# Graph layer, first aggregation: the three histogram steps and the transposes are issued at other places of the tile

## The reference, cut to what matters

```
src = concat(edges[:, 0], edges[:, 1]);  dst = concat(edges[:, 1], edges[:, 0])
deg = segment_sum(ones, dst)             # how many edges end at each node
deg = maximum(deg, 1.0)
agg = segment_sum(x[src], dst) / deg[:, None]
```

## Time and profile before

| | |
|---|---|
| median of 3 runs | 2717.78 us (2715.9 to 2719.15) |
| the profiled execution | 2714.45 us, of which its span is 2712.4 us |
| first aggregation in the trace | from about 509 us to about 1295 us |
| TensorE busy over the span | 2209.7 us (81%) |
| VectorE busy over the span | 1646.6 us (61%) |
| mean granted TensorE clock | 0.955 |

### The profile page before, as it was taken

One profiled execution on the slowest core, in us unless ns is written; L12 is line 12 of the kernel. 1 busy time (PEld: TensorE's weight loads), 2 busy tenths in 40 slices (PEclk: granted clock), 3 DMA queues, 4 the chain that ended last, 5 costly groups with the idle time before them and its releaser, 6 DMA issues.

```text
span 2712.4 us, 51544 instructions
## 1 busy us (share of the span) xinstructions
PE 2209.7 (81%) x15108; PEld 1359.0 (50%) x15109; DVE 1646.6 (61%) x4628; ACT 909.4 (34%) x1775; POOL 272.7 (10%) x368
## 2 busy tenths in 40 slices
PE   3556666599999999999899997999999968999900
PEld 2444444355555555555455553444444437888800
DVE  6999998687887888788332322444444444555533
ACT  1122221245455544545444442111111114555400
POOL 1000000100000000000110100111111120000076
PEclk9999998899999999999899998999999988999955
DMA  2111110022222222222221214444445534222244
GB/s 76 31 30 35 34 33 29 39 106 98 106 104 103 106 98 106 100 106 104 81 89 44 73 47 167 181 181 180 180 180 181 182 132 166 91 89 93 85 149 135
DMA packets 122211, 281.61 MB, mean 104 GB/s; under 512 B 29659, under 2 KB 65340, under 8 KB 119972
## 3 DMA queue, kind: packets, MB, share of 16 engines
q1 hardware_dynamic: 107107, 230.04, 23.4%
q0 software_dynamic: 15040, 50.81, 5.6%
HBM read 149.42 MB, written 131.33 MB: 104 GB/s over the span
## 4 chain that ended last, share of the span: by engine, by line
PE 49%; DVE 17%; issue 16%; DVEq 7%; POOL 4%; POOLq 2%; ACT 1%; DMA 1%; SPq 1%; ACTq 0%
PE bank L1931 31%; DVE big L1155 6%; PE bank L2141 6%; PE bank L2127 5%; PE bank L1922 3%; POOL big L865 3%; DVEq L1014 2%; POOLq L752 2%; DVE big L1001 2%; DVE big L991 1%; ACT big L1646 1%; DVEq L1020 1%; DVEq L1000 1%; PE bank L2111 1%; DVEq L987 1%
## 5 line engine op out<-in xcount | busy, mean ns | idle before, releaser
L1931 PE MATMUL bank<-RW,big 128*128 128x512 f16 (+1 forms) x4900 | 1180.3, 380 | 0.0
L1931 PEld LDWEIGHTS bank<-RW,big 128*128 128x128 f16 x4900 | 443.9, 98 | 396.2 <-issue 3.6
L1641 ACT ACTIVATE big<-bank 128x512 f16<-128x512 f32 (+1 forms) x640 | 372.0, 581 | 404.9 <-PE bank L1922 404.7
L1155 DVE TENSOR_TENSOR big<-iotaB,keys 128x512 f16<-128x512 f16 x1300 | 456.9, 419 | 24.8 <-PE bank L1922 16.9
L1922 PE MATMUL bank<-big 128*128 128x128 f16 x2560 | 248.3, 219 | 12.0 <-DVE big L1155 11.8
L1922 PEld LDWEIGHTS bank<-big 128*128 128x128 f16 x2560 | 190.9, 98 | 123.9 <-DVE big L1155 13.0
L1764 ACT ACTIVATE big<-bank,b1A,iscA 128x256 f32<-128x256 f32 x224 | 114.4, 561 | 153.5 <-PE bank L2127 153.5
L2127 PE MATMUL bank<-big,RW 128*128 128x256 f16 x1344 | 156.9, 274 | 0.5 <-issue 0.5
L2141 PE MATMUL bank<-RW,big 128*128 x1344 | 156.4, 273 | 0.0
L1807 PE MATMUL bank<-big 128*128 128x100 f16 x980 | 88.8, 282 | 66.4 <-issue 63.7
L2127 PEld LDWEIGHTS bank<-big,RW 128*128 x1344 | 132.1, 98 | 16.5 <-issue 0.7
(11 more groups left out here) (363 smaller groups left out, 2576.0 us busy)
## 6 DMA issues: line engine op xcount, KB each, us to landing
big<-a_dram SPq DMA_DIRECT2D x49, 832.0 KB
big<-a_dram SPq DMA_DIRECT2D x49, 768.0 KB, 4.3
a_dram<-big SPq DMA_DIRECT2D x49, 640.0 KB, 3.0
a_dram<-big SPq DMA_DIRECT2D x49, 512.0 KB, 2.6
a_dram<-big SPq DMA_DIRECT2D x49, 448.0 KB, 2.5
big<-rows_dram SPq DMA_DIRECT2D x56, 256.0 KB, 2.6
y_dram<-big SPq DMA_DIRECT2D x56, 256.0 KB, 2.0
big<-in_x_dram SPq DMA_DIRECT2D x96, 128.0 KB, 2.1
```

Source lines behind the costliest of these rows:

```text
L1155: last = v.tensor_tensor(out[q].rearrange("p b (m k) -> p b m k", k=2), inturn(iotaB[:, :], QB, P // 2), twice(kd[:, q * QB:(q + 1) * QB, ...
L1641: a.activation(Ab[q][:, 0:n], banks[BB(q)][:, 0:n], ACT.Copy).then_inc(s_ab, 1)
L1931: last = mm(bank[:, :], blk(q, c), src, start=(u == 0), stop=(u == T))
```

## The change

Five conditions in the two hand-written orders are changed; no instruction is added, removed or altered. With q the step after which a piece is issued:

| piece | engine | before | after |
|---|---|---|---|
| `paired` (mask) | VectorE | 5 | 2 |
| `fold` | TensorE | 4 | 5 |
| `spread` | VectorE | 8 | 7 |
| `degrees` (sum) | TensorE | 7 | 8 |
| `degree` (reciprocal) | VectorE | 11 | 10 |
| `transposed` of the previous tile | TensorE | 10 | 11 |

`hist` stays behind step 1 of TensorE.

```diff
 # VectorE, tile1
-                        if q == 5:
+                        if q == 2:
                             paired(early)
-                        if q == 8:
+                        if q == 7:
                             spread(early)
-                        if q == 11:
+                        if q == 10:
                             degree(early)
 # TensorE, tile1
                     if q == 1:
                         hist(t)
-                    if q == 4:
+                    if q == 5:
                         fold(t)
-                    if q == 7:
+                    if q == 8:
                         degrees(t)
-                    if q == 10 and last:
+                    if q == 11 and last:
                         transposed(t - 1)
```

## The result

The changed kernel takes 2648.26 us (four runs, 2646.12 to 2650.37) where the kernel before takes 2716.84 (four, 2715.69 to 2719.15): a ratio of 0.9747, 95% interval 0.973 to 0.9763, 68.6 us less. The forecast was 2649.8, from 68 us less than the 2717.78 that three runs of the kernel before had given. The profiled execution of the changed kernel is the slowest of its four, 2650.37 us with a span of 2647.7.

The account below looks back on a forecast made before the run. TensorE was taken as the bound, idle only while `fold` waits for VectorE's mask; 48 tiles times 1.42 to 1.43 us is 68 us, so the median goes from 2717.78 to 2649.8 us, range 2643 to 2662.

Parts of the forecast that it names:

- One wait: Aggregation tiles 1 to 48: TensorE's `fold` waits for VectorE's mask, 59.7 us in 48 times, its only wait there.
- the upper bound: Wait of `fold`: at most 1.41 + 0.04 = 1.45 us a tile, a gain of 69.6 us over 48 tiles.
- the middle: Wait of `fold`: 1.42 to 1.43 us a tile taken, the middle of the upper two values, 68 us over 48 tiles.
- The small matmuls: The two matmuls of `fold` on TensorE: 0.09 us for the pair when nothing waits, 0.045 each.
- its layout: Both engines' new order timed from TensorE's first `build` of a tile: next tile at 14.40 us, TensorE never waiting.
- the two handovers called tight: On VectorE's queue: `degrees` to `degree`, about 0.2 us to spare, and transposes to `place1`, about 0.1.
- the one at line 1188: VectorE's `degree` needs TensorE's `degrees`: about 0.2 us to spare; a wait of 0.1 to 0.3 would cost nothing.
- The one at line 1208: VectorE's `place1` at 14.00 needs the transposes, starting at 13.5 and running 0.38 us: about 0.1 us to spare.
- VectorE's room: VectorE before the next tile's `finish1`: ready at 14.42, copied sum lets it start at 15.36, so 0.94 us of cover.
- VectorE does not become the bound: Rival in the aggregation: VectorE becomes the bound, period 14.40 + 0.46, saving 46 us, 2672 us; chance 0.05.
- the clock of the stage: Rival in the aggregation: without pauses TensorE drops to clock 0.50, a tile taking 28.1 us, 2732 us; chance 0.015.
- the second rival: Aggregation: the wait only moves, 1.43 us idle reappearing under another name, time staying 2718 us; chance 0.015.

Follow-up runs that it names:

- mask_only: Kernel before with only the mask moved, from after step 5 to after step 2 of VectorE's pairs: 2668.16 us, ratio 0.9814.
- dve_only: Kernel before with VectorE's three moves alone (mask after 2, `spread` after 7, `degree` after 10), TensorE's order as before: 2644.15 us, ratio 0.9737.
- pe_only: Kernel before with TensorE's three moves alone (`fold` after 5, `degrees` after 8, transposes after 11), VectorE's order as before: 2667.89 us, ratio 0.981.
- extra1: Changed kernel with one more 128x512 comparison on VectorE in each tile at step 11, into an unread spare buffer: 2650.06 us, ratio 0.9754.
- mask_at6: Changed kernel with the mask moved from step 2 to step 6 of VectorE's pairs: 2698.38 us, ratio 0.9934.

## Why the prediction was right

- **What bounds the stage.** One wait, 59.7 us as recorded, was read as all that separated TensorE from being busy throughout. After the change it is busy 690.24 of 690.24 us. The run with the other four moves shows that they bring nothing by themselves. Beside the mask's move one of them does carry time, `spread` (the late piece in the waits of `mask_only`): without it 17 us of the gain are lost (`mask_only`), with VectorE's three moves none (`dve_only`). The prediction had not priced the moves apart.
- **What the wait costs.** Counting from start to start gave 1.41 us a tile plus 0.04 for a dearer `fold`, 69.6 us as the upper bound; the recorded idle time gave 59.7. The stage lost 69.7 by the windows and 69.6 between first and last `build`. The upper bound was the right one, and taking the middle cost the prediction 1.6 us. `pe_only` and `mask_only` show both parts apart: 0.32 late where 0.16 are recorded, 0.28 late where nothing is. That the median fell within 1.5 us of the forecast is partly luck, since runs of one kernel spread by some 4 us.
- **The small matmuls.** In the changed kernel the two of `fold` start 0.03 us apart, and the next `build` starts 0.05 behind the second: 0.08 for the pair, where the prediction took 0.09. That 0.01, with rounding, is what its layout has too much, a period of 14.40 where 14.38 was measured. The Trainium skill (TensorE: Matmul & The Clock Gate, "Wait — 56ns, not 53.3ns?") gives about 25 ns from start to start as the first floor of a small matmul. The distance between the two agrees with it; the 0.08 of the pair is nearer to the prediction's 0.09 than to the 0.05 estimated from that floor, and the second floor, about 62 ns, is not seen here.
- **The order on VectorE.** The start of every piece in the new tile came out within 0.06 us. Of the two handovers called tight, the one at line 1188 held: it waits in the first tile alone, where TensorE was held up, for 1.0 us. The one at line 1208 did not. The prediction called it 0.1 us to spare, reckoning with the transposes' 0.38 us of duration and with 1.24 us from the last pairs to `place1`. But `place1` starts 0.55 behind the start of the transposes, and the 1.24 already had some 0.08 of such a wait in it (831.30 to 831.89, 0.59 where 0.51 is enough). So `place1` comes at 13.51 + 0.55 = 14.06, 0.15 late. It costs nothing, as the prediction said of a wait of 0.1 to 0.3 there.
- **VectorE's room.** Forecast 0.94 us a tile; the wait for the copied sum is 42.1 / 48 = 0.88 as recorded. The whole room is larger, 1.11 us from start to start, with the 0.15 at `place1` in it: three runs agree on that, with one more comparison, with four, and with `hist` at 4. One comparison fits in; of four 0.88 us stick out in a steady tile.
- **The rivals.** VectorE does not become the bound (`extra1`), the wait does not move to TensorE again (list of waits), and the clock of the stage stayed at 1.00. But the second rival named a real danger, which the change avoids by moving `spread` too: with the mask alone moved, a quarter of the gain (17 of 69.6 us) went to the next handover.
- **Where the range sat.** The profiled execution should have taken 2646.5 us and took 2650.37. Its first `build` came 4.3 us later than in the trace of before (514.0 against 509.7), with identical code ahead of it. The stage itself was 1.6 us shorter than forecast, so 5.5 us have to be accounted for. These 4.3 are most of it; the rest lies behind the stage and outside the span. Why the first `build` came later is open. The other three runs of the changed kernel took 2646.12 to 2649.92.

## What to carry to other kernels

Where two engines hand pieces back and forth inside a hand-written order, lay out both queues in time from the rows and list for each handover how long the piece is ready before it is due; the sum of what is late on the bounding engine is the price. Moving either end by one step buys one step of the engine on which it is moved: 1.09 us for `fold` (late by 1.41, then 0.32), 0.68 for the mask (from 0.32 in `pe_only` to 1.00 in `mask_at6`). After such a move look at the next handover in the chain, which may now be the late one. A wait on the other engine costs nothing as long as its own work for one round is shorter than the round and no piece that it hands over comes late by it. The first alone is not enough: before the change VectorE's work was shorter than the round, and TensorE still waited for the mask.

## What the hardware showed that was not expected

- A wait for TensorE can be missing from its matmul rows: 0.28 us late from start to start had no idle time at line 1952, and in the list of waits it stood only at the weight load (26.8 us in 44 times). Recorded idle of 1.25 stood for 1.41, and 0.16 for 0.32; the difference is 0.16 each time, by which the four `apply` matmuls' recorded 1.03 us exceeds the 0.86 to the next start (0.17). Of the 0.28 that leaves 0.11, below the smallest idle time that the timelines list here, 0.15. VectorE's wait at `place1` stays unlisted in the same way.
- A small matmul that has been waited for holds TensorE longer than one that has not: 0.13 against 0.08 us for the two of `fold`, 0.10 against 0.03 for the one of `degrees`. The cause was not tried. The weight loads are waited for too (line 1946's 83.4 us in 48 times in the kernel before), but no run shows that they make the difference.
